# Three banks in turn for the MLP tiles, a running sum for the mean, and a new order, in a linear-attention block with two MLPs

## The chip, the cores and the metric

The kernel runs on one core of a Trainium2 chip. The time is device microseconds of one execution. The profile is of one further execution. The core has TensorE (PE, with its weight loads as PEld), VectorE (DVE), ScalarE (ACT), GpSimd (POOL) and SyncE (SP, which issues the DMAs here). PSUM has eight banks of 128 x 512 fp32.

## The reference

```python
def layernorm(x):  # over the last axis
    return (x - mean(x)) / sqrt(var(x) + 1e-5)

x = x0                                              # 8 images x 512 rows x D = 256
# first part, on n = layernorm(x)
u = layernorm(n) * ln1_w + ln1_b
Q, K = elu(u @ q_w.T + q_b) + 1, elu(u @ k_w.T + k_b) + 1   # F = 64 features
V = u @ v_w.T + v_b
attn = causal: sum over j <= i of (Q_i . K_j) V_j, divided by sum over j <= i of (Q_i . K_j) + 1e-6
a = n + attn @ o_w.T + o_b
a = a + gelu((layernorm(a) * ln2_w + ln2_b) @ f1_w.T + f1_b) @ f2_w.T + f2_b   # H = 1024
x = x + a
# second part
h = gelu(layernorm(x) @ ternary(W_fc).T)            # H = 1024
h = layernorm(h) * ln_w + ln_b                      # over the 1024
x = x + h @ ternary(W_proj).T
# ternary(W) = sign(W) * min(round(|W| / mean|W|), 1)
```

## The kernel before

The kernel works image by image (g = 0 to 7, 512 rows each, as four tiles t of 128 rows). Activations and weights are cut into a high and a low part for the fp32r matmuls, so that a product is three matmuls (`split3`), or two where the weight is ternary. For one image the steps are:

- the two first norms and the transposed, scaled input; `qk_mm`, `scores`, `v_mm`, and `attend(g, t)` for four tiles, with `attn_out` on VectorE and the second norm behind it; `tz2(g, h)` transposes the normed rows, two tiles at a time (h = 0, 1);
- the first MLP, eight tiles m of 128 hidden features by 512 rows: `f1(g, m)` (lines 286 to 288) into an MLP bank, `gelu` (ACT, L785) and `h_hi` (ACT, L794), `h_lo` (DVE, L1101), then `f2(g, m, h)` adds into bank_y; `f1h` is half of an f1;
- the third norm, and `tz3(g, h)` (L294), its transposes;
- the second MLP: `fc(g, m)` (L519; `fch` is half of one), on ScalarE `gelu3` (L810), `square` (L836) and `g_hi` (L824), on VectorE `g_lo` (L1269), on GpSimd `sq_add` (L1449), which adds up the squares of the eight tiles, and `proj(g, m)` (L548), which multiplies g_hi and g_lo by the ternary weight and adds into four banks;
- the last norm is applied after the projection: out = rstd * (projection - mean * column sums) + ... The sum of squares is transposed by `tsq` (L560) and reduced by `h2_sum` (L1221). The sum itself, for the mean, comes out of the projection: two extra columns of its weight (columns 256 and 257) hold the high and low part of one over the norm's weight, so that g times them is the plain h. `h_sum` (L1231) adds the two. Since the weight may be zero, `used_weights` on VectorE puts 1 in such a place and `wpj_mask` on GpSimd (L1456) clears the rows of the projection for it. `centre` (L1262) and `ln4_var` follow on VectorE, `ln4_rstd` and `output` on GpSimd, `store` on SyncE.

The MLP tiles of f1 and fc, and tz3, alternate over two banks, f0 and f1. f1(m) waits for h_lo(m-2), fc(m) for g_lo(m-2) and square(m-2). The projection's outputs lie in y0, y1, p and a0. `centred(g-2)` and `h2_total` must be done before `scores(g)`, as they share banks. The last image's second half of tz3 goes into a1.

The work of one image is laid over that of the next: during fc and proj of image g, `attend(g+1, 3)` and `tz2(g+1)` are done, and so on. Each of the five engines has its list of steps, written out by hand in a function `order()` of its own. An engine does its list in that order and waits at each step for semaphores, so a step that waits holds everything behind it in that list. Tiles of `squares` (eight of 128 x 512) take the squares; RG = 3 tiles hold g_hi and g_lo in turn.

Of the kernel before, what the change touches and what calls it, by code (L numbers as in the profile page):

```python
# [21 lines left out]
def build(nc, x, xt_d, wqk_d, wv_d, wo_d, f1_d, f2_d, fc_d, pj_d, vec_d, rows_d, out):  # L22
# [14 lines left out]
    with ExitStack() as ctx:  # L37
# [9 lines left out]
        bank_p, bank_q = bank["p"], bank["a2"]  # L47
# [36 lines left out]
        def by_k(b):  # L84
# [8 lines left out]
        wpj = sb("wpj_t", [P, KH, D + 2], F32R)  # L93
# [74 lines left out]
        squares = h3[:].rearrange("p t f -> p (t f)").rearrange("p (m n) -> p m n", m=KH)  # L168

# [21 lines left out]
        def _(sp):  # L191
# [91 lines left out]
        def _(pe):  # L283
# [49 lines left out]
            def theta_sum(w):  # L333
                pe.wait_ge(s["abs_summed"], 2 * w + 2)
                if w == 0:
                    pe.wait_ge(s["sums_w"], 2)
                    pe.wait_ge(s["v_lo"], 2)
                else:
                    pe.wait_ge(s["xa_ready"], 4)
                pe.matmul((bank_y[1], bank_p)[w][:, 0:2], mean_w[:], abs_sum[:, 2 * w:2 * w + 2],  # L340
                          start=True, stop=True).then_inc(s["theta_sum"], 1)

            def cpj():
# [3 lines left out]
                pe.wait_ge(s["wvo_sum"], 2)  # L347
                for k in range(KH):
                    mm = pe.matmul(bank_p[0:4, 0:D], ln3_split[:, k, :], wpj[:, k, 0:D],
                                   start=(k == 0), stop=(k == KH - 1))  # L350
                mm.then_inc(s["cpj_done"], 1)

            def spread():
                pe.wait_ge(s["rows_ready"], 1)
                pe.wait_ge(s["select_ready"], 3)
                for r in range(2):
                    mm = pe.matmul(bank_p[:, r * D:(r + 1) * D], row_select[:, r, :], pj_rows,
# [36 lines left out]
            def scores(g):  # L394
# [3 lines left out]
                if g >= 2:  # L398
                    pe.wait_ge(s["centred"], 4 * (g - 2) + 4)
# [51 lines left out]

            def f1_wait(g, m):
                if g == 0 and m == 0:
                    pe.wait_ge(s["wf1_lo"], 4)
                if m >= 2:
                    pe.wait_ge(s["h_lo"], 8 * g + m - 1)
                elif g:
                    pe.wait_ge(s["g_lo"], 8 * (g - 1) + m + 7)
                    pe.wait_ge(*squared(g - 1, m + 6))

            def f1(g, m):
                f1_wait(g, m)
                pe.wait_ge(s["z2_lo"], 2 * g + 2)
                for k in range(KD):
                    mm = split3(bank_f[m % 2][:], [w[:, k, m * P:(m + 1) * P] for w in wf1],
# [3 lines left out]
            def f1h(g, m, h):  # L469
# [4 lines left out]
                for k in range(KD):  # L474
                    mm = split3(bank_f[m % 2][:, cols], [w[:, k, m * P:(m + 1) * P] for w in wf1],
# [3 lines left out]
            def f2(g, k, h):  # L479
                pe.wait_ge(s["h_lo"], 8 * g + k + 1)  # L480
                if k == 0:
# [3 lines left out]
                    elif g:  # L485
                        pe.wait_ge(s["centred"], 4 * (g - 1) + h + 1)
                    else:
                        pe.wait_ge(s["wf2_lo"], 4)
                        pe.wait_ge(s["f1_bias_ready"], 1)
                        pe.wait_ge(s["theta_ready"], 1)  # L490
# [1108 lines left out]
```

## Time and profile before

| | us |
|---|---|
| three timed runs | 459.22, 461.87, 462.12 (median 461.87) |
| the profiled execution | 459.8 |
| its span in the profile | 458.1 (1.7 lies around it) |
| TensorE busy | 426.1, 2878 matmuls |
| ScalarE busy | 329.2 |
| VectorE busy | 325.6 |
| GpSimd busy | 304.0 |
| DMA | 20.41 MB, mean 45 GB/s |

The span starts with the first instruction and ends with the last store. Times in the rows below are in microseconds from its start. A group of rows that names one line of code can hold the work of a helper for many steps; the names of the tiles tell which.

### The profile page before, as it was taken

The numbers are of one execution on the slowest core, as the hardware profiler recorded it, in microseconds if no ns is written. First come the engines' busy times: TensorE is split into PE (matmuls) and PEld (weight loads), VectorE is DVE, ScalarE is ACT, GpSimd is POOL, SyncE is SP. The second block draws the span as 40 slices with busy tenths as digits, with TensorE's granted clock in tenths as the row PEclk, the third lists the DMA queues.
The fourth block names the chain that finished last, engine by engine and source line by source line (L and its number), as shares of the span: only waits on it lengthen the run. The fifth ranks groups of instructions, "written<-read, shape, count | busy, mean of one in ns | idle before, by whom it ended". The sixth has DMA issues, their size and how long they took to land.

```text
span 458.1 us, 9001 instructions
## 1 busy us (share of the span) xinstructions
PE 426.1 (93%) x2878; PEld 386.4 (84%) x2878; DVE 325.6 (71%) x1123; ACT 329.2 (72%) x579; POOL 304.0 (66%) x270
## 2 busy tenths in 40 slices
PE   3996999999999999999898999999999999999692
PEld 3886898999989998998888898998899898789682
DVE  6696898559865877658885588586874768544736
ACT  3798557987498758987488767978597757963490
POOL 2786019993878977884599685882778575750294
PEclk9997999999999999999999999999999999999998
DMA  7261001001302130100410301111000001000011
GB/s 247 110 230 47 1 2 47 2 12 36 93 24 70 47 85 10 47 1 1 140 46 2 92 5 44 47 49 35 13 1 24 24 1 46 2 1 1 1 46 47
DMA packets 13519, 20.41 MB, mean 45 GB/s; under 512 B 2720, under 2 KB 11040, under 8 KB 12960
## 3 DMA queue, kind: packets, MB, share of 16 engines
q1 hardware_dynamic: 13472, 19.84, 13.8%
q8 instruction: 23, 0.38, 0.3%
q14 instruction: 24, 0.20, 0.1%
HBM read 15.62 MB, written 4.22 MB: 43 GB/s over the span
## 4 chain that ended last, share of the span: by engine, by line
PE 26%; issue 10%; POOL 10%; DVE 3%; ACT 3%; DMA 1%; POOLq 0%; DVEq 0%; SPq 0%; ACTq 0%
PE bank_f L519 5%; POOL h L1449 3%; PE bank_f L286 2%; PE bank_f L287 2%; PE bank_f L288 2%; PE bank_y L548 2%; PE bank_y L286 2%; PE bank_y L287 2%; PE bank_y L288 2%; POOL rs L1425 2%; POOL y_yc L1506 1%; POOL centred L1503 1%; PE bank_a L548 1%; PE bank_p L548 1%; PE bank_a L286 1%
## 5 line engine op out<-in xcount | busy, mean ns | idle before, releaser
L1449 POOL TENSOR_TENSOR h<-h 128x512 f32<-128x512 f32 x56 | 72.3, 1291 | 8.7 <-ACT h L836 3.8
L1269 DVE SCALAR_TENSOR_TENSOR g_lo<-bank_f,w_used,g_hi 128x512 fp32r<-128x512 f32 x64 | 48.0, 749 | 39.4 <-ACT h L836 20.4
L785 ACT ACTIVATE bank_f<-bank_f,f_bias 128x512 f32<-128x512 f32 x64 | 42.2, 661 | 30.7 <-PE bank_f L288 29.7
L1101 DVE TENSOR_TENSOR h_lo<-bank_f,h_hi 128x512 fp32r<-128x512 f32 x60 | 41.0, 688 | 32.3 <-ACT h_hi L794 32.2
L286 PE MATMUL bank_y<-wf_hi,h_hi 128*128 128x256 f32 x224 | 63.5, 283 | 0.0
L288 PE MATMUL bank_y<-wf_hi,h_lo 128*128 128x256 f32 x224 | 62.9, 281 | 0.0
L287 PE MATMUL bank_y<-wf_lo,h_hi 128*128 128x256 f32 x224 | 62.9, 281 | 0.0
L519 PE MATMUL bank_f<-z3T_hi,wfc_t 128*128 128x512 f32 (+1 forms) x160 | 57.5, 374 | 5.4 <-DVE g_lo L1269 4.2
L286 PE MATMUL bank_f<-z2T_hi,wf_hi 128*128 128x512 f32 (+1 forms) x160 | 58.2, 364 | 2.2 <-DVE z2T_lo L1101 2.0
L287 PE MATMUL bank_f<-z2T_lo,wf_hi 128*128 128x512 f32 (+1 forms) x160 | 56.9, 356 | 0.0
L288 PE MATMUL bank_f<-z2T_hi,wf_lo 128*128 128x512 f32 (+1 forms) x160 | 56.8, 355 | 0.0
L519 PE MATMUL bank_f<-z3T_lo,wfc_t 128*128 128x512 f32 (+1 forms) x160 | 53.7, 349 | 0.0
L1425 POOL TENSOR_TENSOR rs<-ve,neg_half 128x2 f32<-128x2 f32 x32 | 22.5, 702 | 46.7 <-DVE ve L1038 45.3
L810 ACT ACTIVATE bank_f<-bank_f 128x512 f32<-128x512 f32 x64 | 37.8, 590 | 14.6 <-PE bank_f L519 14.0
L824 ACT ACTIVATE g_hi<-bank_f,w_used 128x512 fp32r<-128x512 f32 x64 | 43.8, 686 | 0.7
L286 PEld LDWEIGHTS bank_y<-wf_hi,h_hi 128*128 128x128 f32 x224 | 42.2, 188 | 1.5 <-DVE h_lo L1101 0.4
L287 PEld LDWEIGHTS bank_y<-wf_lo,h_hi 128*128 128x128 f32 x224 | 42.2, 188 | 0.7
L288 PEld LDWEIGHTS bank_y<-wf_hi,h_lo 128*128 128x128 f32 x224 | 42.2, 188 | 0.0
L519 PEld LDWEIGHTS bank_f<-z3T_hi,wfc_t 128*128 128x128 f32 x160 | 30.0, 188 | 13.2 <-DVE g_lo L1269 8.3
L836 ACT ACTIVATE h<-bank_f 128x512 f32<-128x512 f32 x64 | 38.0, 596 | 0.9
L794 ACT ACTIVATE h_hi<-bank_f 128x512 fp32r<-128x512 f32 x60 | 35.6, 596 | 4.2 <-issue 1.3
L286 PEld LDWEIGHTS bank_f<-z2T_hi,wf_hi 128*128 128x128 f32 x160 | 31.2, 195 | 6.4 <-issue 1.5
(329 smaller groups left out, 1353.7 us busy)
## 6 DMA issues: line engine op xcount, KB each, us to landing
out<-y_yc SPq DMA_DIRECT2D x15, 256.0 KB, 2.3
u<-in_xt SPq DMA_DIRECT2D x6, 512.0 KB, 3.4
lines_b<-lines SPq DMA_DIRECT2D x6, 512.0 KB, 4.1
x_even<-in_x SPq DMA_DIRECT2D x8, 256.0 KB, 2.8
x_odd<-in_x SPq DMA_DIRECT2D x8, 256.0 KB, 3.3
h<-in_f SPq DMA_DIRECT2D x1, 1024.0 KB, 7.6
y_yc<-in_f SPq DMA_DIRECT2D x1, 1024.0 KB, 9.9
h<-in_fc SPq DMA_DIRECT2D x1, 1024.0 KB, 5.9
```

Of the source, the lines that this page charges most:

```text
L286: pe.matmul(ps, w[0], r[0], start=start, stop=False, skip_group_check=skip)
L287: pe.matmul(ps, w[0], r[1], start=False, stop=False, skip_group_check=skip)
L288: return pe.matmul(ps, w[1], r[0], start=False, stop=stop, skip_group_check=skip)
L519: mm = pe.matmul(bank_f[m % 2][:, cols], wfc[:, k, m * P:(m + 1) * P], z3T[part][:, k, cols], start=(k == 0 and part == 0), stop=(k == KD ...
L785: act.activation(bank_f[m % 2][:], bank_f[m % 2][:], ACT.Gelu, bias=f1_bias[:, m:m + 1]).then_inc(s["h_gelu"], 1)
L794: act.activation(h_tile(0, g, m), bank_f[m % 2][:], ACT.Copy).then_inc(s["h_hi"], 1)
L810: act.activation(bank_f[m % 2][:], bank_f[m % 2][:], ACT.Gelu).then_inc(s["h3_ready"], 1)
L824: act.activation(gr[0][:, n % RG, :], bank_f[m % 2][:], ACT.Copy, scale=w_used[:, m:m + 1]).then_inc(s["g_hi"], 1)
L836: act.activation(squares[:, m, :], bank_f[m % 2][:], ACT.Square).then_inc(squared(g, m)[0], 1)
L1101: dve.tensor_tensor(dst, b, hi.bitcast(F32), ALU.subtract).then_inc(s[ready], 1)
L1269: dve.scalar_tensor_tensor(gr[1][:, n % RG, :], bank_f[m % 2][:], w_used[:, m:m + 1], gr[0][:, n % RG, :].bitcast(F32), ALU.mult, ALU.subt ...
L1449: pool.tensor_tensor(squares[:, 0, :], squares[:, 0, :], squares[:, m, :], ALU.add).then_inc(s["squares_sum"], 1)
```

## The change

- The bank p joins f0 and f1 in a ring of three: f1(m) in ring[m % 3], tz3(h) in ring[(8+h) % 3], fc(m) in ring[(10+m) % 3]. f1 and fc wait for the tile three back. Since the mean no longer comes from the projection, "tile free" is g_lo and the new h_add.
- The projection is 256 columns wide and its four outputs lie in the two halves of y0 and y1. Two things that used p move: the column sums of the projection (`cpj`, `spread`) into y0, the second theta sum beside the first in y1.
- `h_add(g, m)` on VectorE adds each gelu tile into a running sum `h_sums`, which lies in the last tile of `squares` (the square of m = 7 takes tile 1 instead). `ths(g)` on TensorE transposes it into a0, and `h_sum` reduces that in one operation of 128 x 512. `used_weights`, `inv_hi`, `inv_lo` and `wpj_mask` go.
- `attn_out` is three steps now: attn_den, attn_rec, attn_out.
- f2(g, 0, h) waits for two tiles of centre, not one, and f2(0, 0) for the second theta too; scores(g) waits for `h_total` of g-2 instead of `centred`; theta_sum(1) for the first theta; proj(g, 0) no longer for xa.
- The lists of all five engines are new. At the start: ScalarE's table load stands first; qk_mm(1) ahead of the attends of image 0, scores(1) and v_mm(1, 0) ahead of the first f1h. In the middle: tz3(g) among attend(g+1), g_lo and h_add next to each other. At the end: proj(7, 6), ths(7), tsq(7), proj(7, 7) on TensorE; output(6, *) earlier among the sq_add of image 7 on GpSimd; centre of image 7 after ln4_var on VectorE.

```diff
-        def z3_bank(g, h):
-            return bank_a[1] if (g, h) == (G - 1, 1) else bank_f[h]
-        def out_bank(t):
-            return (bank_y[0], bank_y[1], bank_p, bank_a[0])[t]
+        ring = bank_f + [bank["p"]]
+        def f1_bank(m):
+            return ring[m % 3]
+        def z3_bank(h):
+            return ring[(8 + h) % 3]
+        def fc_bank(m):
+            return ring[(10 + m) % 3]
+        def out_half(t):
+            return bank_y[t // 2][:, (t % 2) * D:(t % 2 + 1) * D]
...
+            def fc_tile_free(g, m):
+                pe.wait_ge(s["g_lo"], 8 * g + m + 1)
+                pe.wait_ge(s["h_added"], 8 * g + m + 1)
             def f1_wait(g, m):
...
-                if m >= 2:
-                    pe.wait_ge(s["h_lo"], 8 * g + m - 1)
+                if m >= 3:
+                    pe.wait_ge(s["h_lo"], 8 * g + m - 2)
                 elif g:
-                    pe.wait_ge(s["g_lo"], 8 * (g - 1) + m + 7)
-                    pe.wait_ge(*squared(g - 1, m + 6))
+                    fc_tile_free(g - 1, m + 5)
...
             def tz3(g, h):
                 pe.wait_ge(s["z3_ready"], 4 * g + 2 * h + 2)
...
-                    pe.wait_ge(s["h_lo"], 8 * g + 7 + h)
+                pe.wait_ge(s["h_lo"], 8 * g + 6 + h)
             def fc_wait(g, m):
...
-                if m >= 2:
-                    pe.wait_ge(s["g_lo"], 8 * g + m - 1)
-                    pe.wait_ge(*squared(g, m - 2))
+                if m >= 3:
+                    fc_tile_free(g, m - 3)
...
             def proj(g, m):
...
-                        mm = pe.matmul(out_bank(t)[:, 0:D + 2], gr[part][:, (8 * g + m) % RG, t * P:(t + 1) * P],
-                                       wpj[:, m, :], start=(m == 0 and part == 0), stop=(m == KH - 1 and part == 1))
+                        mm = pe.matmul(out_half(t), gr[part][:, (8 * g + m) % RG, t * P:(t + 1) * P], wpj[:, m, :],
+                                       start=(m == 0 and part == 0 and t % 2 == 0), stop=(m == KH - 1 and part == 1),
+                                       skip_group_check=True)
...
+            def ths(g):
+                pe.wait_ge(s["h_added"], 8 * g + 8)
+                pe.wait_ge(s["xa_ready"], 4 * min(g + 1, G - 1) + 2)
+                for t in range(T):
+                    mm = pe.transpose(bank_a[0][:, t * P:(t + 1) * P], h_sums[:, t * P:(t + 1) * P], ident[:])
+                mm.then_inc(s["hs_done"], 1)
...
-                for t in range(T):
-                    dve.wait_ge(s["pj_tile"], 4 * g + t + 1)
-                    dve.tensor_reduce(h_total[:, t:t + 1], out_bank(t)[:, D:D + 2], AXX, ALU.add).then_inc(s["h_total"], 1)
+                dve.wait_ge(s["hs_done"], g + 1)
+                dve.tensor_reduce(h_total[:], bank_a[0][:].rearrange("p (t f) -> p t f", t=T),
+                                  AXX, ALU.add).then_inc(s["h_total"], 1)
...
+            def h_add(g, m):
+                n = 8 * g + m
+                dve.wait_ge(s["g_hi"], n + 1)
+                dve.wait_ge(s["squared"], n + 1)
+                if m:
+                    dve.wait_ge(s["h_added"], n)
+                    dve.tensor_tensor(h_sums, fc_bank(m)[:], h_sums, ALU.add).then_inc(s["h_added"], 1)
+                    return
...
+                dve.tensor_scalar(h_sums, fc_bank(m)[:], 1.0, None, ALU.mult).then_inc(s["h_added"], 1)
```

TensorE's new list, around the start, a middle image and the end:

```python
qkb(); tu(0, 0); tu(0, 1); wvo_mm(); qk_mm(0); bvo(); fill(); tu(1, 0); v_mm(0, 0); v_mm(0, 1)
tu(1, 1); scores(0); qk_mm(1); attend(0, 0); attend(0, 1); attend(0, 2); attend(0, 3); f1b()
scores(1); theta_sum(0); tz2(0, 0); tz2(0, 1); v_mm(1, 0); f1h(0, 0, 0); f1h(0, 0, 1); f1h(0, 1, 0)
f1h(0, 1, 1); f1(0, 2); v_mm(1, 1); f1(0, 3); f1(0, 4); theta_sum(1); f1(0, 5); f2(0, 0, 0)
...
f2(3, 7, 1); v_mm(4, 0); v_mm(4, 1); attend(4, 0); tz3(3, 0); attend(4, 1); tz3(3, 1); attend(4, 2)
fch(3, 0, 0); fch(3, 0, 1); fch(3, 1, 0); fch(3, 1, 1); fc(3, 2); attend(4, 3); proj(3, 0); fc(3, 3)
proj(3, 1); fc(3, 4); tz2(4, 0); fc(3, 5); proj(3, 2); proj(3, 3); fc(3, 6); proj(3, 4); fc(3, 7)
proj(3, 5); tz2(4, 1); f1h(4, 0, 0); proj(3, 6); f1h(4, 1, 0); f1h(4, 0, 1); f1h(4, 1, 1); f1(4, 2)
ths(3); proj(3, 7); f1(4, 3); f1(4, 4); f1(4, 5); qk_mm(5); f2(4, 0, 0); f2(4, 1, 0); f2(4, 0, 1)
...
fc(7, 4); fc(7, 5); proj(7, 2); fc(7, 6); proj(7, 3); fc(7, 7); proj(7, 4); proj(7, 5); proj(7, 6)
ths(7); tsq(7); proj(7, 7)
```

## Rows read from the trace of the kernel before

**Rows 1.** The page: busy us of each engine, share of the span, instructions.

```profile
PE 426.1 (93%) x2878; PEld 386.4 (84%) x2878; DVE 325.6 (71%) x1123; ACT 329.2 (72%) x579; POOL 304.0 (66%) x270
```

**Rows 2.** Busy time by stretch; then granted clock, DMA share, GB/s.

```profile
0.00:23.00 23.00, 15.60 (x71) 13.33 (x72) 15.03 (x67) 11.96 (x22) 12.13 (x19) 1.00 0.53 178
23.00:45.20 22.20, 17.79 (x119) 16.65 (x119) 18.78 (x78) 19.64 (x38) 16.86 (x15) 0.85 0.42 143
...
98.00:427.00 329.00, 321.50 (x2213) 292.58 (x2212) 234.71 (x802) 244.82 (x426) 226.26 (x196) 1.00 0.12 35
427.00:450.00 23.00, 18.37 (x119) 15.76 (x117) 13.06 (x47) 15.17 (x26) 15.95 (x14) 1.00 0.07 24
```

**Rows 3.** Timeline of TensorE: start, duration, line, tile. Ten, sixteen and eight apart.

```profile
46.62 0.40 PE L287 MATMUL bank_f<-z2T_lo,wf_hi 128*128 128x512 f32 x1
...
48.96 0.40 PE L288 MATMUL bank_f<-z2T_hi,wf_lo 128*128 128x512 f32 x1
49.19 0.28 PE L286 MATMUL bank_y<-wf_hi,h_hi 128*128 128x256 f32 x1
...
51.08 0.28 PE L287 MATMUL bank_y<-wf_lo,h_hi 128*128 128x256 f32 x1
...
445.24 0.28 PE L548 MATMUL bank_p<-wpj_t,g_hi 128*128 128x258 f32 x1
...
446.19 0.29 PE L548 MATMUL bank_p<-wpj_t,g_hi 128*128 128x258 f32 x1
```

**Rows 4.** Timeline of TensorE: the first half of tz3, images 2 and 6.

```profile
173.48 0.66 PE L294 MATMUL bank_f<-ident,z 128*128 128x128 f32 x4 [0.73 <-ACT z L683]
...
380.38 0.65 PE L294 MATMUL bank_f<-ident,z 128*128 128x128 f32 x4 [0.73 <-ACT z L683]
```

**Rows 5.** Timeline of TensorE in image 3: in brackets the idle time before.

```profile
226.08 0.66 PE L294 MATMUL bank_f<-ident,z 128*128 128x128 f32 x4 [1.31 <-ACT z L683]
226.49 0.37 PE L286 MATMUL bank_a<-v_hi,ae_hi 128*128 128x258 f32 x1
...
242.03 0.50 PE L519 MATMUL bank_f<-z3T_hi,wfc_t 128*128 128x512 f32 x1 [1.17 <-DVE g_lo L1269]
```

**Rows 6.** Waits over the whole span: us in total, times, longest.

```profile
DVE g_lo L1269 <- ACT h L836: 20.4, 21, 1.9
...
ACT bank_f L810 <- PE bank_f L519: 14.0, 15, 1.6
...
PEld bank_f L519 <- DVE g_lo L1269: 8.3, 15, 2.0
```

**Rows 7.** Timeline of ScalarE, image 3's fc stage: one gelu3 and the next.

```profile
228.92 0.58 ACT L810 ACTIVATE bank_f<-bank_f 128x512 f32<-128x512 f32 x1 [1.56 <-PE bank_f L519]
...
230.60 0.60 ACT L810 ACTIVATE bank_f<-bank_f 128x512 f32<-128x512 f32 x1
```

**Rows 8.** Timeline of VectorE: 128x512 operations back to back.

```profile
26.84 0.68 DVE L1101 TENSOR_TENSOR ad_lo<-bank_f,ad_hi 128x512 fp32r<-128x512 f32 x1
27.44 0.68 DVE L1101 TENSOR_TENSOR v_lo<-bank_y,v_hi 128x512 fp32r<-128x512 f32 x1
```

**Rows 9.** Busy time by stretch, image 3's fc stage; columns as in rows 2.

```profile
226.00:250.00 24.00, 22.70 (x161) 20.77 (x162) 18.01 (x69) 19.61 (x37) 20.24 (x18) 1.00 0.17 51
```

**Rows 10.** The first f1h: timeline of TensorE, then the stretch it lies in.

```profile
39.56 0.55 PE L286 MATMUL bank_f<-z2T_hi,wf_hi 128*128 128x256 f32 x1 [1.26 <-DVE z2T_lo L1101]
39.91 0.41 PE L287 MATMUL bank_f<-z2T_lo,wf_hi 128*128 128x256 f32 x1
...
40.76 0.41 PE L288 MATMUL bank_f<-z2T_hi,wf_lo 128*128 128x256 f32 x1
...
40.00:44.00 4.00, 4.00 (x21) 4.00 (x21) 2.33 (x11) 2.90 (x5) 3.52 (x3) 0.50 0.40 131
```

**Rows 11.** Timeline of the last stage: GpSimd's squares sums, TensorE's tsq(7).

```profile
440.56 8.47 POOL L1449 TENSOR_TENSOR h<-h 128x512 f32<-128x512 f32 x6
...
449.08 0.66 PE L560 MATMUL bank_a<-ident,h 128*128 128x128 f32 x4 [0.28 <-POOL h L1449]
```

More of the change, by code:

```diff
@@ L1351, in order @@
[L1351 to L1353 removed]
+                consts(); ln1_stats(0, 0); ln1_stats(0, 1); dcol(); ln1_shift(0, 0); u_odd(0, 0); ln1_shift(0, 1)
+                u_odd(0, 1); wide_cols(); n1_ve(0); u_lo(0, 0); n1_shift(0); wqk_lo(); u_lo(0, 1); ln1_stats(1, 0)
@@ new lines, in order @@
+                g_lo(0, 2); h_add(0, 2); ln2_stats(1, 3); h_add(0, 3); g_lo(0, 3); z2_lo(1, 0); ln2_var(1, 1)
+                g_lo(0, 4); g_lo(0, 5); ln2_shift(1, 1); h_add(0, 4); h_add(0, 5); g_lo(0, 6); n1_shift(2)
+                h_add(0, 6); z2_lo(1, 1); g_lo(0, 7); h_add(0, 7); h_lo(1, 0); h_sum(0); centre(0, 0); centre(0, 1)
+                centre(0, 2); h_lo(1, 1); h_lo(1, 2); qk_max(2); qk_sum(2); centre(0, 3); ln1_stats(3, 0)
+                ln1_stats(3, 1); qk_lo(2); h_lo(1, 3); h_lo(1, 4); h2_sum(0); ln4_var(0); ae_mask(2); h_lo(1, 5)
@@ new lines, in order @@
+                g_lo(1, 2); h_add(1, 2); attn_rec(2, 2); attn_out(2, 2); g_lo(1, 3); ln2_shift(2, 0); h_add(1, 3)
+                ln2_stats(2, 2); g_lo(1, 4); attn_den(2, 3); attn_rec(2, 3); attn_out(2, 3); h_add(1, 4)
+                ln2_stats(2, 3); ln2_var(2, 1); g_lo(1, 5); ln2_shift(2, 1); g_lo(1, 6); h_add(1, 5); z2_lo(2, 0)
+                h_add(1, 6); h_add(1, 7); z2_lo(2, 1); g_lo(1, 7); n1_shift(3); h_sum(1); h_lo(2, 0); h_lo(2, 1)
+                ln1_stats(4, 0); centre(1, 0); centre(1, 1); h_lo(2, 2); centre(1, 2); qk_max(3); qk_sum(3)
@@ new lines, in order @@
+                g_lo(4, 5); h_add(4, 4); ln2_shift(5, 1); h_add(4, 5); g_lo(4, 6); z2_lo(5, 0); h_add(4, 6)
+                z2_lo(5, 1); h_add(4, 7); g_lo(4, 7); h_lo(5, 0); h_sum(4); h_lo(5, 1); qk_max(6); h_lo(5, 2)
+                centre(4, 0); qk_sum(6); centre(4, 1); centre(4, 2); n1_shift(6); centre(4, 3); ln1_stats(7, 0)
+                h_lo(5, 3); qk_lo(6); h2_sum(4); ln4_var(4); ae_mask(6); ad_mask(6); h_lo(5, 4); ln1_stats(7, 1)
+                af_mask(6); ad_lo(6); h_lo(5, 5); ln1_shift(7, 0); ln1_shift(7, 1); af_lo(6); n1_ve(7); h_lo(5, 6)
@@ new lines, in order @@
+                n1_shift(7); attn_rec(6, 3); h_add(5, 3); g_lo(5, 3); attn_out(6, 3); ln2_stats(6, 3); ln2_var(6, 1)
+                g_lo(5, 4); ln2_shift(6, 1); h_add(5, 4); h_add(5, 5); g_lo(5, 5); z2_lo(6, 0); z2_lo(6, 1)
+                h_add(5, 6); g_lo(5, 6); g_lo(5, 7); h_add(5, 7); qk_max(7); h_lo(6, 0); h_lo(6, 1); h_sum(5)
+                centre(5, 0); centre(5, 1); qk_sum(7); h2_sum(5); centre(5, 2); centre(5, 3); ln4_var(5); h_lo(6, 2)
+                qk_lo(7); h_lo(6, 3); ad_mask(7); af_mask(7); h_lo(6, 4); h_lo(6, 5); ae_mask(7); ae_lo(7); h_lo(6, 6)
```

593 lines of the change are left out of this document (275 added, 318 removed).

## The prediction, made before the changed kernel had run

> **What bounds the kernel now.** I read the page's shares first: TensorE is busy for 93% of the span and its weight loads for 84%, the other engines for 66 to 72% [rows 1]. A busy TensorE can still be a stalled one, since matmuls overlap, so the next view was the table by stretch [rows 2]. Two stretches stand out: from 23 to 45.2 us TensorE is busy for 17.8 of 22.2 us at a granted clock of 0.85, and from 427 to 450 for 18.4 of 23.0. In the 329 us between, it is idle for 7.5 only. The last transposes end at 449.7 [rows 11], 8.4 us before the span does.
>
> What the middle really loses comes from start-to-start times [rows 3]: ten matmuls of 512 columns take 2.34 us (0.234 each), sixteen of 256 columns 1.89 (0.118), eight of 258 columns 0.95 (0.119). The four transposes of a 128x512 tile take 0.41 [rows 5]. An image has 48 + 32 + 24 / 2 + 6 matmuls of 512 columns or their worth (f1, fc, v_mm, qk_mm: 98, or 22.9 us), 96 of 256 (f2: 11.3), 64 of 258 (proj: 7.6), 30 of 258 in attend (3.6), the scores (2560 columns: 1.2) and five tiles of transposes (2.1). That is 48.7 us. The same transpose of images 2 and 6 starts 206.9 us apart [rows 4], so an image takes 51.7. The middle loses 3.0 us for each image, and the table's 1.2 (7.5 over 6.4 images) is the part that shows as idle.
>
> Where the 3.0 go is in the waits [rows 5, 6]. The first is tz3: its bank is one of the two MLP banks, its data is late, and nothing stands between (1.31 us before the first transpose of image 3). The second is fc on g_lo (1.17 us before one of image 3's tiles; the weight loads of L519 waited 8.3 us in 15 cases). ScalarE in turn waits for fc 14.0 us. It is a circle of two banks: a tile of fc is written (0.94), read by gelu3, square and g_hi on ScalarE (the next gelu3 starts 1.68 after) and by g_lo on VectorE (0.6 more) [rows 7], 3.2 in all; the hand-overs between the engines make it about 4.2 (estimate: four of some 0.25, by the 1.17 that fc waited). Two banks give one tile each 2.1 us, while TensorE needs 4 x 0.234 + 8 x 0.119 = 1.89 for fc and proj of one tile. That is a stage bound by its banks by a little.
>
> **The change, part by part.** The sum is made against the profiled execution, 459.8 us (span 458.1 and 1.7 around it). The three timed runs have their median at 461.9, so that one execution is quick; the four times together have their middle at 460.8, and I add 1 to the sum at the end.
>
> *Third bank.* A tile may now be held for three turns. With h_add it is held 0.6 longer, 4.8 us, and 4.8 / 3 = 1.6 us is under the 1.89 that TensorE needs: the circle stops binding. tz3 no longer waits for a bank and is set among the attend matmuls in the new order, so that its late data costs less. I take 1.5 of the 3.0 us for each image; the rest are hand-overs at other places that nothing here touches. Bounds: nothing, if ScalarE or VectorE simply sets the pace, and the whole 3.0. Over 6.4 images: -9.6 (0 to -19, of which I believe no more than -14).
>
> *Columns and transposes.* 512 proj matmuls go from 0.119 to 0.118 at the rows, 258 to 256 columns, by proportion 0.001 each: -0.5 (0 to -1.5). ths adds 8 x 0.41 = +3.3 on TensorE. It stands behind proj or f1 work, so its own wait for h_added(7) should be over; if it isn't, everything on TensorE queues behind it, one g_lo and one h_add (1.3 us) per image. Together +2.8.
>
> *h_add on VectorE.* 64 operations of 128x512; back-to-back ones of that size start 0.60 apart [rows 8]: 38 us added to an engine busy for 326 of 458. They lie beside TensorE's work as long as VectorE has room. In the stretch of image 3's fc stage, VectorE is busy for 18.0 of 24.0 us, ScalarE 19.6, TensorE 22.7 [rows 9]. With eight h_adds, 4.8 us, VectorE comes to 22.8, as much as TensorE has. The new order moves other VectorE work (row statistics of the next image, centre) out of that stage, so I take nothing on the path; without that cover it costs up to 4.8 us an image. The small reduces of h_sum, used_weights and the two inverse columns leave VectorE and are not counted. A 128x512 reduce for each image comes. g_lo and h_add both wait for g_hi and square; behind them in VectorE's queue stand z2_lo and the next stage's h_lo, for which f1 and f2 wait.
>
> *Start.* f1h(0) stands after idle time: 1.26 us before it, and its matmuls of 256 columns start 0.213 apart at a granted clock of 0.50, the lower level, 1.2 GHz, until 44 us [rows 10]. The new order puts scores(1) and v_mm(1,0) (eight matmuls with 2560 columns in all, 1.2 us at the pace of the rows, and 12 of 256, 1.4 us) into that gap, ahead of f1h(0), and brings qk_mm(1) forward. I count 2.6 for work already done by then, 0.4 for an earlier start (f1b is taken out of its way), and 24 x (0.213 - 0.118) = 2.3 for the clock that stays at the upper level: -5.3. Against that, ternaries and both thresholds stand among the h_lo of image 0, and f2(0,0) now waits for the second theta: +1.0, an estimate (two ternaries of the four ahead of the h_lo that f2 needs). Together -4.3 (0 to -7). wpj_mask, two operations on GpSimd, goes; it lies beside other work. The loads and stores in new order on SyncE's queue cost nothing in the middle (DMA engines busy for 12% there).
>
> *End.* ScalarE sets the last fc stage, and that stays. Six squares sums on GpSimd take 8.47 us and tsq(7) waits for the last [rows 11]; the order now has output(6,*) earlier among them, so the last one ends sooner: -1 (+1 to -1.5). ths(7) is put ahead of tsq(7), waiting for h_add(7,7), which VectorE does before g_lo(7,7). It has room there.
>
> Sum: -9.6 + 2.8 + 0 - 4.3 - 1 = -12.1, so 447.7, and with the 1 for the middle of the runs 448.7.
>
> A row and a rule side by side: the rows of fc and tz3 show the same gap in every image. The Trainium skill (Perfetto Trace Analysis, Optimization Strategy) says that a bubble which repeats on the engine that should be full can mean too few PSUM tiles, which by this trace would give the forecast's sum. The same page (Identifying the Most-Contended Engine) says to judge TensorE not by its matmul share and to work on the engine that is fullest; the weight loads' 84% are here above VectorE's 71%, and by that rule a change that adds work to TensorE should lose the 2.8 us and gain only in gaps. That is the first rival.
>
> **The rivals.**
>
> *The ring frees nothing.* The stalls go to other places: with a third bank ScalarE is the next limit of the fc stage (19.6 of 24.0 [rows 9]), its gelu3, square and g_hi, plus the norms, come as late as before, and h_add holds each bank 0.6 longer. For it: fc's waits end with g_lo [rows 6], and g_lo itself waited 20.4 us for square. Against it: ScalarE waited 14.0 us for fc. Then 459.8 - 4.3 + 2.8 = 458.3, with the 1 some 459.3: within 1%.
>
> *VectorE becomes the bound (slower).* Its queue of the fc stage takes longer than TensorE's. Place: from z3_lo(g) to h_add(g,7) and z2_lo(g+1). By the same stretch [rows 9] it needs 22.8 of 24.0 us if nothing is moved out; with its own waits (20.4 us for square alone [rows 6], over 326 busy) it would reach only some nine tenths of full (estimate), 22.8 / 0.9 = 25.3, or +1.3 for each image over today's 24. It decides once VectorE's queue for the stage passes 22.7, TensorE's. Then 459.8 + 8 x 1.3 + 2.8 - 4.3 = 468.7, with the 1 some 470. Against it: statistics, centre and h_sum can lie in the MLP1 stage, where VectorE has only h_lo of each tile.
>
> *The start gives nothing back:* f1h(0) waits for z2_lo as before and the clock falls all the same: +4 on the forecast, 452.7. It is inside the range.
>
> **How the numbers follow.** The forecast has 0.60, the start that gives nothing 0.13, the ring that frees nothing 0.15, VectorE as the bound 0.12. What a measurement of this kernel can tell from no change is about 1%, 4.6 us. Faster by more than that: the forecast and the third case, 0.73, and a little of the second (0.02): 0.75. Within 1%: 0.14. Slower: 0.11. The predicted time is the forecast's. The range goes from 440 (ring at -14, columns at -1.5, start at -7, the rest as taken: 459.8 + 1 - 14 + 1.8 - 7 - 1 = 440.6) up to 460, which takes in the ring that frees nothing and leaves out the VectorE case (0.12) and a little at the lower end.
>
> **What would show it.** Right: waits of L519 on g_lo and h_add of 2 us or less in all; the start-to-start period of images 2 to 6 near 50.4; the granted clock 1.00 from 36 to 44 us; VectorE at some 365 us. Wrong: TensorE waiting at f1 or fc for L1269 or the new h_add line as long as now (VectorE's case); ScalarE without idle time in the fc stage and the same period, 51.7 (the ring's); the clock at 0.50 somewhere before 50 us (the start's).

## The result and the profile after

| | us |
|---|---|
| four runs of the changed kernel | 448.52, 448.90, 450.07, 450.32 (median 449.49) |
| four runs of the kernel before, beside them | 459.22, 461.38, 461.87, 462.12 (median 461.62) |
| ratio | 0.9746 (95% interval 0.9705 to 0.9788) |
| profiled execution after | 450.3, span 448.5 |

The changed kernel is faster by 12.1 us in the medians, 2.5%. The two profiled executions lie 9.5 us apart, since that of before was a quick one of its kind and that of after the slowest of its four. By the runs side by side the gain is 12.1 us (9.8 to 13.6 by the interval of the ratio). In the later sets of runs, of 13 each, the kernel before had medians of 460.2 to 460.4; against those, 449.5 is 10.8 less.

The head of the page of the changed kernel (columns as in rows 1):

```profile
PE 425.4 (95%) x2910; PEld 388.0 (87%) x2910; DVE 361.1 (81%) x1156; ACT 324.6 (72%) x578; POOL 300.5 (67%) x268
```

VectorE is 35.5 us busier than in rows 1 and the kernel is shorter all the same. TensorE has its 32 transposes more and is busy for a greater share. Busy time by stretch of the changed kernel, columns as in rows 2:

```profile
23.00:45.20 22.20, 20.44 (x148) 18.71 (x147) 19.26 (x63) 19.40 (x36) 14.90 (x14) 1.00 0.35 120
...
45.20:98.00 52.80, 50.94 (x336) 46.01 (x336) 44.98 (x133) 37.71 (x70) 31.24 (x27) 0.97 0.11 31
98.00:420.00 322.00, 318.08 (x2230) 291.98 (x2229) 259.55 (x834) 237.93 (x423) 225.56 (x196) 1.00 0.11 34
```

Against rows 2: in the same 22.2 us of the start TensorE starts 148 matmuls instead of 119, at a clock of 1.00 instead of 0.85. From 45.2 to 98 it gives a part back (336 against 363 before): it now stands still there for 1.9 us and runs at 0.97. In the middle it idles 3.9 of 322 us, where it was 7.5 of 329.

Timeline of TensorE of the changed kernel, the first half of tz3 of images 1, 2 and 6 (answers to rows 4), and of the last matmul:

```profile
119.59 0.60 PE L300 MATMUL bank_p<-ident,z 128*128 128x128 f32 x4
...
170.12 0.66 PE L300 MATMUL bank_p<-ident,z 128*128 128x128 f32 x4 [0.76 <-ACT z L695]
...
373.53 0.66 PE L300 MATMUL bank_p<-ident,z 128*128 128x128 f32 x4
...
440.39 0.27 PE L551 MATMUL bank_y<-wpj_t,g_lo 128*128 128x256 f32 x1
```

Before, the same three transposes started at 122.5, 173.5 and 380.4 us (the first is not in rows 4). So the changed kernel is ahead by 2.9, 3.4 and 6.8 us, and by 9.6 at the end of the span. From image 2 to image 6 an image takes (373.53 - 170.12) / 4 = 50.85 us, where it took 51.7: 0.87 less for each.

The waits over the span of the changed kernel, those that answer to rows 6:

```profile
ACT bank_f L822 <- PE bank_f L525: 11.0, 10, 2.1
DVE g_lo L1263 <- ACT h L851: 7.1, 11, 2.3
```

The wait of fc's weight loads for g_lo, 8.3 us in 15 cases in rows 6, stands at 0.9 for the banks f0 and f1 and at 0.2 for p in the groups by line. VectorE's waits for square ahead of g_lo fell from 20.4 to 7.1; its h_adds wait another 1.1 for square and 1.9 for g_hi.

### The profile page after: what moved, and what is told of

It is laid out like the page before. It is cut to its first block and busy times, and to the rows that moved or that the text cites. A ratio compares the mean times of both kernels' runs of the same rounds, so it can differ in the third digit from the quotient of the medians.

```text
span 448.5 us, 9187 instructions
## 1 busy us (share of the span) xinstructions
PE 425.4 (95%) x2910; PEld 388.0 (87%) x2910; DVE 361.1 (81%) x1156; ACT 324.6 (72%) x578; POOL 300.5 (67%) x268
## 5 line engine op out<-in xcount | busy, mean ns | idle before, releaser
L292 PE MATMUL bank_y<-wf_hi,h_hi 128*128 128x256 f32 x224 | 63.4, 283 | 0.8 <-DVE h_lo L1091 0.6
L551 PE MATMUL bank_y<-wpj_t,g_hi 128*128 128x256 f32 x256 | 63.3, 284 | 0.1
L551 PE MATMUL bank_y<-wpj_t,g_lo 128*128 128x256 f32 x256 | 62.2, 280 | 0.0
L551 PEld LDWEIGHTS bank_y<-wpj_t,g_hi 128*128 128x128 f32 x256 | 48.1, 188 | 2.2 <-issue 0.5
L551 PEld LDWEIGHTS bank_y<-wpj_t,g_lo 128*128 128x128 f32 x256 | 48.2, 188 | 1.2
L797 ACT ACTIVATE bank_f<-bank_f,f_bias 128x512 f32<-128x512 f32 x48 | 31.6, 662 | 20.0 <-PE bank_f L294 19.6
L292 PE MATMUL bank_f<-z2T_hi,wf_hi 128*128 128x512 f32 (+1 forms) x128 | 44.8, 350 | 0.4 <-DVE h_lo L1091 0.3
L292 PEld LDWEIGHTS bank_y<-wf_hi,h_hi 128*128 128x128 f32 x224 | 42.1, 188 | 2.5 <-DVE h_lo L1091 1.5
L294 PE MATMUL bank_f<-z2T_hi,wf_lo 128*128 128x512 f32 (+1 forms) x128 | 43.3, 339 | 0.0
L293 PE MATMUL bank_f<-z2T_lo,wf_hi 128*128 128x512 f32 (+1 forms) x128 | 43.3, 338 | 0.0
L525 PE MATMUL bank_f<-z3T_hi,wfc_t 128*128 128x512 f32 (+1 forms) x96 | 36.0, 381 | 1.7 <-DVE z3T_lo L1091 1.7
L1263 DVE SCALAR_TENSOR_TENSOR g_lo<-bank_f,vec,g_hi 128x512 fp32r<-128x512 f32 x40 | 29.8, 746 | 7.3 <-ACT h L851 5.2
L525 PE MATMUL bank_f<-z3T_lo,wfc_t 128*128 128x512 f32 (+1 forms) x96 | 34.5, 365 | 0.0
L822 ACT ACTIVATE bank_f<-bank_f 128x512 f32<-128x512 f32 x40 | 23.7, 595 | 11.1 <-PE bank_f L525 11.0
```

Source lines behind the costliest of these rows:

```text
L292: pe.matmul(ps, w[0], r[0], start=start, stop=False, skip_group_check=skip)
L293: pe.matmul(ps, w[0], r[1], start=False, stop=False, skip_group_check=skip)
L294: return pe.matmul(ps, w[1], r[0], start=False, stop=stop, skip_group_check=skip)
L525: mm = pe.matmul(fc_bank(m)[:, cols], wfc[:, k, m * P:(m + 1) * P], z3T[part][:, k, cols], start=(k == 0 and part == 0), stop=(k == KD - 1 ...
L551: mm = pe.matmul(out_half(t), gr[part][:, (8 * g + m) % RG, t * P:(t + 1) * P], wpj[:, m, :], start=(m == 0 and part == 0 and t % 2 == 0), ...
L797: act.activation(f1_bank(m)[:], f1_bank(m)[:], ACT.Gelu, bias=f1_bias[:, m:m + 1]).then_inc(s["h_gelu"], 1)
```

## The experiments

All ratios are against the kernel before run beside them on the same chip; its medians there were 460.2 to 460.4. The changed kernel wasn't run again in these sets: its 449.5 and its ratio of 0.975 are those of the result, beside a median of 461.6. So a difference of about 1 us between it and an experiment can't be told from a difference between the sets, and where one is small the time of one image in the traces is given too.

### The new order without the third bank's freedom

```diff
-                if m >= 3:
-                    fc_tile_free(g, m - 3)
+                if m >= 2:
+                    fc_tile_free(g, m - 2)
...
-                if m >= 3:
-                    pe.wait_ge(s["h_lo"], 8 * g + m - 2)
+                if m >= 2:
+                    pe.wait_ge(s["h_lo"], 8 * g + m - 1)
...
-                    fc_tile_free(g - 1, m + 5)
+                    fc_tile_free(g - 1, m + 6)
...
-                pe.wait_ge(s["h_lo"], 8 * g + 6 + h)
+                pe.wait_ge(s["h_lo"], 8 * g + 7 + h)
```

> The changed kernel with everything new kept (ring of three banks, running sum, new order), but fc waits for the tile two back and so does f1 (for 7 of its tiles, where the new order of the other engines forbids it, it stays at three back), and tz3 waits one h_lo longer: the third bank can be written, but TensorE may not run ahead into it. If the third bank is what frees the middle (the forecast): the cycle of a fc tile, held for some 4.8 us with the added sum, over two banks is 2.4 us against TensorE's 1.89, so about +0.3 to +0.5 for each of 64 fc tiles: 470 or more, slower than the kernel before. If the ring frees nothing and the order alone made the gain: within 2 us of the changed kernel's 449.5. In between if the other engines' orders already hide most of it.

(The second of these edits leaves out seven of the f1 tiles, which stay at three back.) Measured: 590.1 us, ratio 1.283 (1.278 to 1.288). That is 141 us more than the changed kernel, more than the 0.3 to 0.5 for each of 64 fc tiles of the expectation. Its waits (TensorE's largest at fc, L527, and at f1, L292):

```profile
PE bank_f L527 <- DVE g_lo L1265: 38.1, 20, 3.6
PE bank_f L292 <- DVE h_lo L1093: 26.4, 13, 3.6
PE bank_p L292 <- DVE h_lo L1093: 12.6, 9, 2.6
```

With the 4.4 us of its tiles in p, fc waits 42.5 us for g_lo; f1 waits 39.0 for h_lo. So nearly half of the waiting is in the first MLP, and the mean granted clock is 0.939 where the changed kernel has 0.986. The new lists let TensorE take two fc tiles with no proj between them (fc(3, 4); tz2(4, 0); fc(3, 5)) and ScalarE two gelus; with waits for two tiles back, every such pair would be a trip through all the engines. This reason is argued from the lists. The run shows that the new order can't live without the ring. It doesn't show what the ring is worth, so the next four runs take the old lists.

### Ring and order apart

`old_order_ring` has all the new functions, and the lists of before (start included):

```diff
 (lists of the five engines as before, but)
+ VectorE: h_add(g, m) behind each g_lo(g, m); centre(g, 0..3) together
+ VectorE: attn_den, attn_rec, attn_out in place of attn_out
+ TensorE: ths(g) behind proj(g, 7)
- VectorE, ScalarE, GpSimd: used_weights, inv_hi, inv_lo, wpj_mask
```

> All of the change but its order: ring of three banks with waits three back, projection in y0 and y1, running sum, while the five engines' lists are those of the kernel before, with h_add behind each g_lo, ths behind proj(g, 7) and the four centres of an image together (the new waits need that). The start is that of before too. Ring as the cause (forecast): the middle still gains most of its 1.5 us for each image, and only the start's 4 us and the end's 1 are missing: 452 to 456. If the gain is the order's, and the ring alone frees nothing: 460 or more, and with VectorE's 64 additions in an order not made for them up to 470.

> The same kernel as old_order_ring, but f1 and fc wait for the tile two back and tz3 one h_lo longer, as in the kernel before: the running sum without the third bank's freedom. Against old_order_ring it gives the ring's price with nothing else changed. Ring as the cause: at least 10 us above old_order_ring, since each of 64 fc tiles now is held for 4.8 us over two turns, 2.4 against 1.89. If the order is what counts: within 3 us of it.

> old_order_ring (471.0) with the additions on one column instead of 512 (the mean is then wrong; that part of the computation is left out). It gives the ring's value where VectorE isn't loaded. If the additions are what makes the old order slow (VectorE at its limit there): 454 to 458, so the ring is worth 2 to 6 us against the kernel before, and the additions cost some 15. If the old lists don't suit the ring at all (ths, the four centres together): 465 or more, and the additions cost little.

> old_order_two_turns (485.8) with the additions on one column (same part left out). It is nearest to the kernel before: two turns, old order, without the additions' work, but with their waits, ths and the centres together. If the additions cost 0.6 us for each tile that is held longer over two turns: 462 to 466 (2 to 6 above the kernel before for ths and the added waits). If something else in the port of the old lists costs the time: 475 or more.

| lists | tiles back | additions | us | ratio (95%) | an image |
|---|---|---|---|---|---|
| old | two | 512 columns | 485.8 | 1.056 (1.053 to 1.059) | 54.8 |
| old | three | 512 columns | 471.0 | 1.024 (1.019 to 1.029) | 53.0 |
| old | two | one column | 473.7 | 1.026 (1.023 to 1.030) | 53.1 |
| old | three | one column | 464.5 | 1.008 (1.006 to 1.011) | 52.2 |
| new | three | 512 columns | 449.5 | 0.975 (0.971 to 0.979) | 50.9 |
| new | three | one column | 448.4 | 0.974 (0.972 to 0.977) | 50.8 |

The last column is the time of one image in us, from the first half of tz3 of image 2 to that of image 6 in each trace, divided by four; the kernel before has 51.7. (One of the ten executions of the fourth row took 1453.6 us. Nothing here shows why, and the ratio is without it.)

With the old lists the ring is worth 14.8 us with the additions and 9.2 without them, and the additions cost 12.1 us over two banks and 6.5 over three. So it does what the forecast says of it. But all of the change in the old order is 10.8 us slower than the kernel before, and its images take 1.2 us longer. The new lists, with the new start in them, bring 21.5 us on top (471.0 to 449.5), and they take the price of the additions from 6.5 us to 1.1 or less: both kernels with the new lists have the same ratio, and their images differ by 0.1. My expectation for `old_order_ring`, 452 to 456, was too low by 15: I had given the middle's gain to the bank alone. That for `old_order_two_turns`, at least 10 above it, held. The two with one column came out between the cases that I had named for them.

The waits of `old_order_two_turns` and then of `old_order_ring` show the circle of two banks and what is left of it:

```profile
PEld bank_f L525 <- DVE g_lo L1338: 15.3, 11, 4.1
PE bank_f L525 <- DVE g_lo L1338: 11.0, 9, 3.9
```

```profile
PEld bank_y L551 <- DVE g_lo L1338: 9.5, 17, 1.2
...
PEld bank_f L525 <- DVE g_lo L1338: 4.1, 2, 3.4
```

With the ring fc waits for VectorE in 2 cases instead of 11, but now the projection waits for it (L551, 17 times; with two banks no such wait is listed). With the additions on one column this wait is 4.8 us in 10 cases, so the h_add ahead of each g_lo in VectorE's queue makes about half of it. In the changed kernel it is 0.2 us. TensorE's lists differ little in this: the old ones have fc two tiles ahead of proj for most tiles and the new ones two or three. VectorE's differ more. In the 24 us from the first half of tz3 of image 3 it is busy for 22.8 in `old_order_ring` and for 20.3 in the changed kernel:

```profile
228.30:252.30 24.00, 21.29 (x150) 19.01 (x149) 22.82 (x80) 19.70 (x37) 19.81 (x18) 1.00 0.20 56
```

```profile
221.40:245.40 24.00, 24.00 (x174) 22.21 (x172) 20.26 (x56) 20.40 (x38) 21.77 (x19) 1.00 0.06 18
```

The 22.8 is the figure at which the slower rival saw VectorE as the bound. That the wait went mainly because VectorE has less to do there is read from these rows; no run changed VectorE's list alone.

The row with two tiles back and one column is the nearest to the kernel before and is 13 us slower than that. So the way from the kernel before goes +13.2, then -9.2 for the ring, +6.5 for the additions and -21.5 for the lists. What makes up the 13.2 (ths, 3.3 by the rows, the waits of f2 for two centres, the four outputs in two banks that f2 of the next image wants, the one-column operations with their waits) wasn't taken apart.

### How much room VectorE has

`add_one_column` takes the work of the additions out of the changed kernel, `add_twice` doubles it:

```diff
-                    dve.tensor_tensor(h_sums, fc_bank(m)[:], h_sums, ALU.add)
+                    dve.tensor_tensor(h_sums[:, 0:1], fc_bank(m)[:, 0:1], h_sums[:, 0:1], ALU.add)
```

```diff
+                    dve.tensor_tensor(spare[:], fc_bank(m)[:], h_sums, ALU.add)
                     dve.tensor_tensor(h_sums, fc_bank(m)[:], h_sums, ALU.add)
```

> The changed kernel with the running sum's 56 additions on one column instead of 512 (the mean is then wrong; that part of the computation is left out). All waits and semaphores stay. If the additions lie wholly beside TensorE's work, as forecast, the time stays within 1 us of 449.5. If VectorE had become the limit in the fc stages (the slower rival), taking away some 34 us of its work gives back several us: 445 or less.

> The changed kernel with each of the 56 additions of the running sum done twice, the first into a spare tile: 34 us more of VectorE work, all in the fc stages. If VectorE still has room there: within 2 us of 449.5. If the additions already fill it (VectorE busy 22.8 of 24 us by the estimate): each further 0.6 us shows, 56 x 0.6 = 34 us at most, so 465 to 480.

Measured: 448.4 without (1.1 us less), 470.2 with twice the work, ratio 1.023 (1.020 to 1.027), 20.7 us more. The first 34 us of additions cost 1.1 us at most, the next 34 cost 20.7, and an image takes 53.3 us instead of 50.9. The stretch of `add_twice` from the first half of tz3 of image 3:

```profile
229.00:253.00 24.00, 23.16 (x159) 20.41 (x158) 22.43 (x62) 18.53 (x35) 20.58 (x18) 1.00 0.01 2
```

VectorE is busy for 22.4 of 24.0 there, near where the slower rival put the changed kernel (22.8). The changed kernel itself has 20.3, as shown above. The same stretch of the kernel before:

```profile
224.20:248.20 24.00, 21.47 (x152) 19.30 (x151) 19.05 (x73) 19.61 (x37) 20.10 (x18) 1.00 0.20 56
```

So a nearly full VectorE goes with a longer time. The changed kernel stays short of it: by these stretches the new lists have moved some 3.6 us of other VectorE work out of the stage (19.05 + 4.8 - 20.26). One thing isn't separated: the second addition also holds each tile 0.6 us longer, and fc's weight loads wait for g_lo again in `add_twice`, 6.2 us in 7 cases.

### The start

```diff
-                scores(1); theta_sum(0); tz2(0, 0); tz2(0, 1); v_mm(1, 0); f1h(0, 0, 0); f1h(0, 0, 1); f1h(0, 1, 0)
-                f1h(0, 1, 1); f1(0, 2);
+                theta_sum(0); tz2(0, 0); tz2(0, 1); f1h(0, 0, 0); f1h(0, 0, 1); f1h(0, 1, 0)
+                f1h(0, 1, 1); scores(1); v_mm(1, 0); f1(0, 2);
```

and on VectorE ae_mask(1), ae_lo(1), ad_mask(1), af_mask(1), ad_lo(1), on ScalarE ae_hi(1) and ad_hi(1), behind tile 1 of image 0's first MLP.

> The changed kernel with scores(1) and v_mm(1, 0) put back behind the first two f1 tiles, with the masks and low parts of image 1 behind h_lo(0, 1) on VectorE and ScalarE. If the start gains as forecast, by filling the gap before f1h(0, 0, 0) and keeping the clock at the upper level: the granted clock falls to 0.5 after the gap again and the time is 3 to 5 us longer, 453 to 454. If the new start gave nothing: 449 to 450.

Measured: 459.3 us, ratio 0.998 (0.996 to 1.000), 9.8 us more than the changed kernel. That is twice what was expected. Stretches of `start_undone`, then of the changed kernel:

```profile
36.00:40.00 4.00, 3.11 (x17) 2.74 (x16) 1.81 (x6) 2.01 (x4) 3.29 (x3) 0.55 0.27 113
40.00:44.00 4.00, 4.00 (x21) 3.90 (x20) 1.66 (x3) 2.79 (x4) 1.47 (x2) 0.60 0.43 131
44.00:48.00 4.00, 1.01 (x7) 0.81 (x6) 3.34 (x10) 1.31 (x4) 0.00 (x0) 0.83 0.00 0
48.00:52.00 4.00, 4.00 (x16) 3.71 (x16) 0.85 (x2) 0.59 (x1) 0.00 (x0) 0.50 0.01 4
```

```profile
36.00:40.00 4.00, 4.00 (x36) 3.98 (x35) 3.38 (x10) 3.04 (x6) 3.18 (x3) 1.00 0.33 137
40.00:44.00 4.00, 4.00 (x29) 3.72 (x28) 2.31 (x3) 3.89 (x8) 1.64 (x2) 1.00 0.40 135
```

TensorE starts 38 matmuls from 36 to 44 us instead of 65, and its clock falls twice: once in the gap ahead of f1h(0), as before (rows 10), and again behind 44 us, where v_mm(1, 0) waits for ae_lo(1), which now stands late in VectorE's queue (3.0 us of waiting). That second gap isn't in the kernel before, so 9.8 us is more than the new start gains over the old one. In the lists of before the start has no such gap: `old_order_ring` reached tz3(0) at 69.8 us, as before, and not at 78.1 as this kernel. From tz3(0) to the end of the span `start_undone` takes 380.6 us and the changed kernel 380.4, so all of the 9.8 lies in the start. The run shows the mechanism (gap, then low clock) and not its size.

### The projection's columns

```diff
-  out_bank(t)[:, 0:D + 2] ... wpj[:, m, :]
+  out_bank(t)[:, 0:D] ... wpj[:, m, 0:D]
```

> The kernel before with the projection 256 columns wide instead of 258 and nothing else changed (the mean is then wrong; that part of the computation is left out). 512 matmuls are each 2 columns shorter. By the rows, 0.5 us less (0 to 1.5): 459.8 to 460.3 beside 460.3. If the projection's matmuls don't set the pace of their stage, 0.

Measured: 460.2 beside 460.2, ratio 0.9997 (0.998 to 1.002). Two columns less in each of 512 matmuls are worth nothing that shows.

### Two gaps and the small operations

The changed kernel's profile shows two places where TensorE stood and its clock fell after. The first lies behind tz3(0); TensorE's timeline, and then the stretch after it:

```profile
70.25 0.36 PE L525 MATMUL bank_f<-z3T_hi,wfc_t 128*128 128x256 f32 x1 [1.05 <-DVE z3T_lo L1091]
```

```profile
72.00:76.00 4.00, 4.00 (x24) 3.77 (x23) 1.92 (x5) 3.34 (x7) 4.00 (x4) 0.74 0.00 0
```

The second is at the last image's tz3(7, 1) (1.05 us for z3_norm at 420.5).

```diff
-  TensorE: fch(0, 0, 0); fch(0, 0, 1); fch(0, 1, 0); fch(0, 1, 1); fc(0, 2); attend(1, 3); proj(0, 0)
+  TensorE: attend(1, 3); fch(0, 0, 0); fch(0, 0, 1); fch(0, 1, 0); fch(0, 1, 1); fc(0, 2); proj(0, 0)
-  TensorE: tz3(7, 1); fch(7, 0, 0); fch(7, 0, 1); fch(7, 1, 0); fch(7, 1, 1)
+  TensorE: fch(7, 0, 0); fch(7, 1, 0); tz3(7, 1); fch(7, 0, 1); fch(7, 1, 1)
-  ScalarE: z3_norm(7, 0); z3_norm(7, 1); z3_hi(7, 0); z3_hi(7, 1)
+  ScalarE: z3_norm(7, 0); z3_hi(7, 0); z3_norm(7, 1); z3_hi(7, 1)
-  VectorE: ln3_shift(7, 1); z3_odd(7, 1); z3_lo(7, 0); z3_lo(7, 1)
+  VectorE: z3_lo(7, 0); ln3_shift(7, 1); z3_odd(7, 1); z3_lo(7, 1)
```

> The changed kernel with two gaps of TensorE closed, after which its profile shows a lower clock: attend(1, 3) goes ahead of fch(0, 0, 0), where TensorE stood 1.05 us for z3_lo; and for the last image z3_hi(7, 0) goes ahead of z3_norm(7, 1) on ScalarE, z3_lo(7, 0) ahead of the shift on VectorE, and fch(7, 0, 0) and fch(7, 1, 0) ahead of tz3(7, 1). If these gaps cost what they seem (1.1 and some 1.5 of idle time, and half speed for some 3 us after each in part of the executions): 445 to 447. If the chain to gelu3(7, 0) and other engines set the end: 449 to 450.

Measured: 448.9 us, ratio 0.976 (0.973 to 0.978), 0.6 less than the changed kernel's median and inside its spread. That is the second of the two cases that were expected. The granted clock is 1.00 from 68 to 76 us, but TensorE stands somewhere else: behind fc(0, 2) it waits for the g_lo of proj(0, 0).

```profile
68.00:72.00 4.00, 4.00 (x34) 3.76 (x33) 3.64 (x15) 2.96 (x7) 2.22 (x3) 1.00 0.00 0
72.00:76.00 4.00, 3.05 (x20) 2.38 (x19) 2.22 (x6) 3.97 (x9) 4.00 (x4) 1.00 0.00 0
```

```profile
74.53 0.36 PE L551 MATMUL bank_y<-wpj_t,g_hi 128*128 128x256 f32 x1 [0.95 <-DVE g_lo L1263]
```

The gap moved from 70 to 73.6 us, where ScalarE, which makes the g_hi ahead of that g_lo, is busy for 3.97 of 4. By that row ScalarE sets the pace there, though GpSimd is busy throughout as well. It is the same at the end: TensorE now stands 1.50 us ahead of fch(7, 0, 0) and 1.42 ahead of proj(7, 0). Filling one gap opens the next; what remained is a clock that doesn't fall, and two of the changed kernel's own four executions have a mean clock as high (0.996, 448.5 and 448.9 us).

`small_ops_merged` makes one operation of 128x4 of each four of one column in `ln4_var` and `centre`:

```diff
-                for t in range(T):
-                    dve.tensor_scalar(h_mean2[:, t:t + 1], h_total[:, t:t + 1], h_total[:, t:t + 1], -1.0 / (H * H), ...
+                dve.scalar_tensor_tensor(h_mean2[:], h_total[:], -1.0 / (H * H), h_total[:], ...
```

> The changed kernel with the 16 one-column operations of ln4_var and centre (t = 0) of each image made into four operations of 128x4. Behind the last matmul VectorE is busy without a gap up to the last stores, with 1.8 us of it in those operations in the last image: if that is the end's path, 1.0 to 1.4 us less, 448.1 to 448.5. If GpSimd's or the stores' times set the end: within 0.3 of 449.5.

> small_ops_merged and two_gaps_filled together. If the two are independent: 0.6 (the measured gain of the filled gaps) and 1.2 us off 449.5, 447.4 to 448.0, with the granted clock at 1.00 throughout the middle. If they hide each other: as the better of the two.

Measured: 450.1 us, ratio 0.977 (0.974 to 0.980), and together with the filled gaps 449.0, 0.975 (0.972 to 0.977). Neither is faster than the changed kernel by more than the runs spread, and neither gave the 1.0 to 1.4 us that the merged operations were to save on the end's path. VectorE's timeline at the end of `merged_and_filled` says why, with GpSimd's behind it:

```profile
438.41 0.69 DVE L1214 TENSOR_REDUCE h_total<-bank_a 128x4 f32<-128x512 f32 x1
439.02 1.12 DVE L1229 SCALAR_TENSOR_TENSOR h_mean<-h_total 128x4 f32<-128x4 f32 x1
440.35 0.16 DVE L1235 SCALAR_TENSOR_TENSOR ve<-h_total,h_mean 128x4 f32<-128x4 f32 x1 [0.21 <-DVE h_mean L1229]
```

```profile
437.62 2.50 POOL L1510 TENSOR_TENSOR y_yc<-y_yc,pj_rows_b 128x512 f32<-128x512 f32 x2
```

The merged operation takes 1.12 us here and 0.15 to 0.17 in five of its eight cases. It ends at 440.14, where GpSimd's operation ends (440.12). The four one-column operations that it replaced took 0.57. From the start of these operations to the first centred VectorE needs 2.11 us here and 2.05 in `two_gaps_filled`, which has the one-column form: what the other merged operations save is lost in this one. More on this below.

## Why the prediction was right, and where it was not

The time was forecast at 448.7 and is 449.5; the forecast's own sum, -12.1 us, was made against the profiled execution, and between the profiled executions it is -9.5. By its terms:

- **Start, -4.3.** By tz3(1, 0) the changed kernel is 2.9 us ahead in its profiled execution. `add_one_column` has the same lists, and its clock doesn't fall at 68 to 76 us: there it is 4.3 ahead (118.2 against 122.5). The mechanism was right: the clock stays at 1.00 where it was at 0.50 [rows 10]. The term that was mis-sized in the profiled execution is what is given back: 1.0 was put down for ternaries and thresholds. What the trace has is a new gap of 1.05 us ahead of fch(0, 0, 0), and in this execution a low clock behind it.
- **Third bank, -9.6, and h_add at nothing.** The sum of the two is right in this kernel. Images 2 to 6 gain 0.87 each with the transposes counted in (0.41 each), so 1.2 to 1.3 us of the 3.0 were taken away for each image, where 1.5 was forecast. That h_add lies beside other work is right as well: 1.1 us at most for 34. But I gave the whole gain to the bank and took the order as its servant. The runs show that the bank alone doesn't do it: without the new lists the same functions are slower than the kernel before by 10.8 us. The step that failed is "the circle stops binding", taken as enough by itself. The ring is worth 9.2 to 14.8 us in the old lists, but against it stand two prices that the sum has at nothing or not at all: 6.5 us for h_add with VectorE at 22.8 of 24 us, and 13.2 for the rest of the change in the old lists, of which only the 3.3 of ths were forecast.
- **Columns, -0.5:** nothing (-0.0, with 0.9 to either side).
- **Transposes, +3.3:** not run alone. They stand in TensorE's stream at the pace of rows 5.
- **End, -1.** From the last matmul to the end of the span it is 7.8 us instead of 8.4, and tz3(6, 0) to the end is 75.0 instead of 77.7, of which one image's 0.9 belongs to the middle. That is -1.9 all told, 0.4 beyond the bound of -1.5. Counted from tz3(7, 0) alone it is 31.6 us instead of 32.8.

Luck has a part in the number. The sum of -12.1 equals the difference of the medians to the tenth, but between the profiled executions, against which it was made, there are 9.5, and against the later medians 10.8. The start and the middle gave less than forecast in the profiled pair and the end more.

The signs that were to show it right: fc waits for g_lo for 1.1 us in all (2 or less was named), the clock is 1.00 from 36 to 44 us, VectorE is at 361 (some 365), and an image takes 50.85 (near 50.4; the forecast's own terms, 51.7 - 1.5 + 0.4 - 0.1, give 50.5). One row was misread: the transpose at 226.08 us with 1.31 us of idle time ahead of it is the second half of tz3 of image 3 and not its first, which starts at 224.17 without a wait. The sum doesn't use that figure.

The rivals: the ring that frees nothing fell by the ring's 14.8 and 9.2 us in the old lists. VectorE as the bound fell for this kernel by the 1.1 us, and `add_twice` and `old_order_ring` show how near it is. Its condition was a VectorE queue above 22.7 of 24 us in the fc stage; by busy time these two have 22.4 and 22.8, and take 470.2 and 471.0 us, where the rival had 470. That the times agree is chance: the rival's sum starts at the kernel before, without the ring's gain or the prices of the old lists. The Trainium skill (Perfetto Trace Analysis, Optimization Strategy) says that a gap which keeps coming back on the engine that should be full can mean too little SBUF or PSUM for the next tile. The runs agree in part: with the third bank the wait of fc's weight loads for g_lo went from 15.3 to 4.1 us in the old lists, and the kernel was still slower than the one before.

## What to carry to other kernels

A third buffer and the lists that use it are one change: with the old lists the buffer was worth 9 to 15 us and the whole still lost, and the new lists with waits for two tiles back were 141 us slower. Price work that is added to an engine "beside" the bound one by how full that engine will be in that stage: here the additions that brought VectorE to 20.3 of 24 us cost at most 3% of their length, and those that brought it to 22.4 cost 60%. When a gap on the bound engine is filled, look for what ends the stage first, since the gap can simply move.

## What the runs showed of the hardware

Small VectorE operations with two tensors in SBUF can be held up by GpSimd. In `merged_and_filled` the operation of line 1229 reads two SBUF tensors of 128x4 (the same one twice). It took 0.15 to 0.17 us in five of eight cases, in which GpSimd was idle, and 0.77, 0.23 and 1.12 in the other three. In these a GpSimd tensor_tensor of 128x512 ran, and VectorE's operation ended 0.02 to 0.04 us behind the end of it. In the trace of `small_ops_merged` the same three cases took 0.77, 0.61 and 1.12. The first of the three (VectorE, then GpSimd):

```profile
352.07 0.77 DVE L1229 SCALAR_TENSOR_TENSOR h_mean<-h_total 128x4 f32<-128x4 f32 x1
```

```profile
350.27 2.54 POOL L1500 TENSOR_TENSOR y_yc<-y_yc,xa 128x512 f32<-128x512 f32 x2
```

GpSimd's second operation ends at 352.81 here and VectorE's at 352.84. The one-column form with its scalars from a column took 0.20 us at every one of its 32 times in the changed kernel (0.203 to 0.215), though twelve of these ran beside such a GpSimd operation, so four small operations can be quicker than one. The Trainium skill (SBUF — State Buffer, Who interferes with whom) says that VectorE and GpSimd share one pair of SBUF ports under an exclusive lock; the two ends that coincide agree with that. The h_adds, which read one tensor from PSUM and one from SBUF, lay beside GpSimd's squares sums and took 0.68 us on the mean, as other VectorE operations of that size did [rows 8].

The same gap in TensorE's work is followed by a fallen clock in some executions and not in others. Ahead of the first fc it is 1.05 to 1.06 us in four traces with the same lists for TensorE. From 72 to 76 us the granted clock is then 0.74 in the changed kernel and 0.71 in `small_ops_merged`, and 1.00 in `add_one_column` and `add_twice`:

```profile
70.25 0.36 PE L525 MATMUL bank_f<-z3T_hi,wfc_t 128*128 128x256 f32 x1 [1.06 <-DVE z3T_lo L1091]
...
72.00:76.00 4.00, 4.00 (x31) 3.78 (x30) 2.37 (x6) 3.97 (x9) 4.00 (x4) 1.00 0.00 0
```

These two lines are of `add_one_column`; those of the changed kernel stand further up. Its four executions have mean clocks of 0.986 to 0.996, and the two of 0.996 are the two fastest, 1.2 to 1.8 us ahead of the others. Only one of the four has a trace, so where the clock of the others fell isn't shown.
